# A vision tower on one core: values in stationaries of 32 or 64 columns dealt over strips, and half of the key spreading on ScalarE

## The reference

```python
q, k, v = split(x @ Wqkv)                 # H heads of d
att = softmax-like(q @ k.T * scale)       # 26 x 26 for each head
out = (att @ v) @ Wo                      # then added back
```

## Time and profile before

| | |
|---|---|
| median of three runs | 3102.24 us (3101.4 to 3104.73) |
| span of the profiled execution | 3102.3 us |
| TensorE busy | 2887.7 us, 93% |
| VectorE busy | 2090.0 us, 67% |
| ScalarE busy | 1075.2 us, 35% |
| GpSimd busy | 616.9 us, 20% |

### The profile page before, as it was taken

The page is one execution under the profiler, slowest core; times in us unless marked ns, Lnnn a source line. Parts: engine busy times, 40 slices in busy tenths (PEclk is TensorE's granted clock), DMA queues, the critical chain, the costliest instruction groups (busy, mean ns, idle before and its releaser), DMA issues. The chain is left out here.

```text
span 3102.3 us, 56416 instructions
## 1 busy us (share of the span) xinstructions
PE 2887.7 (93%) x19925; PEld 2668.6 (86%) x19925; DVE 2090.0 (67%) x5299; ACT 1075.2 (35%) x2140; POOL 616.9 (20%) x807
## 2 busy tenths in 40 slices
PE   8889999999999999999997998896989889958888
PEld 7789999999999999999997888675778889957677
DVE  3867677777777777777776766333457667777876
ACT  2533333333333333233333333212445333334433
POOL 1312121212112121212112110112213101122450
PEclk9989999999999999999998999798999889989898
DMA  3001100000000000000000000371000100000000
GB/s 136 36 20 37 37 21 33 36 36 18 36 36 36 18 36 36 24 30 36 18 31 9 2 2 2 117 237 54 2 11 2 54 19 19 1 11 16 23 19 17
DMA packets 24461, 105.56 MB, mean 34 GB/s; under 512 B 4455, under 2 KB 9463, under 8 KB 19086
## 3 DMA queue, kind: packets, MB, share of 16 engines
q1 hardware_dynamic: 22654, 99.62, 9.2%
q0 software_dynamic: 1584, 3.30, 0.3%
HBM read 98.32 MB, written 6.64 MB: 34 GB/s over the span
## 5 line engine op out<-in xcount | busy, mean ns | idle before, releaser
L905 ACT ACTIVATE hid<-bank,dat 128x384 f32<-128x384 f32 (+1 forms) x912 | 554.4, 608 | 1147.9 <-PE bank L595 1033.3
L870 PE MATMUL bank<-w,hid_hi 128*128 128x384 f32 x2964 | 857.5, 361 | 2.2 <-DVE y_tok L921 1.6
L872 PE MATMUL bank<-w,hid_lo 128*128 128x192 f32 x2964 | 745.0, 251 | 0.0
L872 PEld LDWEIGHTS bank<-w,hid_lo 128*128 128x128 f32 x2964 | 570.2, 192 | 1.7
L870 PEld LDWEIGHTS bank<-w,hid_hi 128*128 128x128 f32 x2964 | 560.8, 189 | 5.7 <-issue 4.1
L939 DVE TENSOR_TENSOR hid_lo<-hid,hid_hi 128x384 fp32r<-128x384 f32 (+1 forms) x912 | 540.0, 592 | 31.5
L936 DVE CAST hid_hi<-hid 128x384 fp32r<-128x384 f32 (+1 forms) x912 | 340.9, 374 | 126.7 <-ACT hid L905 125.4
L962 DVE SCALAR_TENSOR_TENSOR h_tok<-bank,gate,h_tok 128x192 f32<-128x192 f32 x416 | 173.6, 417 | 246.8 <-PE bank L872 243.3
L595 PE MATMUL bank<-xa_hi,w_hi 128*128 128x384 f32 (+1 forms) x912 | 324.6, 356 | 7.3 <-DVE w_lo L748 4.4
L595 PE MATMUL bank<-xa_lo,w_hi 128*128 128x384 f32 (+1 forms) x912 | 323.2, 354 | 0.0
L595 PE MATMUL bank<-xb,w_lo 128*128 128x384 f32 (+1 forms) x912 | 322.7, 354 | 0.0
(11 more groups left out here) (361 smaller groups left out, 4367.3 us busy)
## 6 DMA issues: line engine op xcount, KB each, us to landing
raw<-in_L_exp SPq DMA_DIRECT2D x36, 1344.0 KB, 5.7
w_e<-in_L_exp SPq DMA_DIRECT2D x20, 576.0 KB, 3.9
w_e<-in_L_exp SPq DMA_DIRECT2D x20, 384.0 KB
pix<-in_pixels SPq DMA_DIRECT2D x6, 832.0 KB, 10.3
w_e<-in_L_exp SPq DMA_DIRECT2D x20, 195.0 KB
raw<-in_L_mlp SPq DMA_DIRECT2D x2, 1344.0 KB, 6.5
wp_raw<-in_L_att SPq DMA_DIRECT2D x1, 2304.0 KB, 8.2
route_rows<-in_rows_clear SPq DMA_DIRECT2D x1, 2000.0 KB, 23.4
```

Source lines behind the costliest of these rows:

```text
L870: nc.tensor.matmul(o[:, 0:2 * D], hid_hi[k % 2][:, m, c], w2[j][:, m, :], start=m == 0, stop=False)
L872: ins = nc.tensor.matmul(o[:, 0:D], hid_lo[k % 2][:, m, c], w2[j][:, m, 0:D], start=False, stop=m == HC - 1)
L905: nc.scalar.activation(hid[(6 * k + m) % 3][:, 0:128 * nt], bank[4 + (6 * k + m) % 4][:, 0:128 * nt], func, bias=bias).then_inc(s["h_act"] ...
```

## The change

Four things.

1. `v_x` keeps a cell of `max(32, d)` columns for each head (32, in relative 64) in place of 128: with d = 16 two heads share 32 output rows, and each cell has its 16 values on its own side. A values instruction has a stationary of one cell and writes only the strip of output rows in which the head belongs, and neighbouring instructions go to different strips. The features of heads 8 to 11, which stand twice, are now computed twice: 16 instructions for 12 heads of 16 (before 12), 8 in causal (before 6), 24 in relative (before 18). The copy of the values into `v_x` is one instruction.
2. Scores and the relative offsets: the loop over chunks is the outer one, the loop over images (strips) the inner.
3. Half of a turn's key spreading, chunks NC/2 and up, moves from VectorE's `spread` to ScalarE, in two parts of three heads (`keys`), with a new semaphore `k_half` that the scores of the turn's first tile wait for. Causal keeps all of it on VectorE.
4. `v_x` is 1536 columns in place of 3200, and its clearing (GpSimd) shrinks with it.

```diff
-        v_x = sb("v_x", [128, 2 * 1536 + 128], scope=at)
+        v_x = sb("v_x", [128, 2 * 768], scope=at)
...
                 order += [("exp", 2, 0), ("bd", 1, 0), ("values", 0, 0), ("v", 2, 0), ("scores", 3, 0)] + kq
-                order += [("exp", 3, 0), ("bd", 2, 0), ("values", 1, 0), ("v", 3, 0)]
+                order += [("exp", 3, 0), ("bd", 2, 0), ("keys", 0, 1), ("values", 1, 0), ("v", 3, 0), ("keys", 1, 1)]
...
-                order = [("k", 0, 1), ("bd", 0, 0), ("mass", 0, 0), ("q", 0, 1), ("scores", 0, 1), ("values", 0, 0),
+                order = [("k", 0, 1), ("bd", 0, 0), ("mass", 0, 0), ("keys", 0, 1), ("q", 0, 1), ("keys", 1, 1), ("scores", 0, 1), ("values", 0, 0),
...
+            cell = max(32, d)
+            in_cell = cell // d
+
+            def value_cell(j, h):
+
+                x0 = 768 * j + cell * h
+                return v_x[:, x0:x0 + cell]
...
                     if g == 0:
                         pe.wait_ge(s["k_done"].sem, b["k_done"] + i + 1)
+                        if cfg.kind != "causal":
+                            pe.wait_ge(s["k_half"].sem, b["k_half"] + i + 1)
                         used(last_qk[0], i, last_qk[1])
                     o = bank[4 + g % 2]
-                    for im in range(4):
-                        m = SLOT * (4 * g + im)
-                        for c in range(NC):
-                            kx = key_rows(i, c * HCH, HCH).rearrange("p (h n) -> p h n", n=n)
+                    for c in range(NC):
+                        kx = key_rows(i, c * HCH, HCH).rearrange("p (h n) -> p h n", n=n)
+                        w = HCH * SLOT
+                        for im in range(4):
+                            m = SLOT * (4 * g + im)
                             q0 = qcols(c, i).start + m
-                            w = HCH * SLOT
...
-                    for im in range(4):
-                        m = SLOT * (4 * g + im)
-                        for c in range(NC):
+                    for c in range(NC):
+                        for im in range(4):
+                            m = SLOT * (4 * g + im)
                             ins = nc.tensor.matmul(o[32 * im:32 * im + 32, 40 * c:40 * c + 40],
...
-                    def product(o, h, start, stop):
-                        x0 = 1536 * (g % 2) + 128 * h
-                        return nc.tensor.matmul(o, v_x[:, x0:x0 + 128], p_bd[g % 2][:, h, :], start=start, stop=stop)
+                    def product(o, h, strip, start, stop):
+
+                        return nc.tensor.matmul(o[cell * strip:cell * strip + cell, :], value_cell(g % 2, h),
+                                                p_bd[g % 2][:, h, :], start=start, stop=stop)
...
-                            for c, hs in enumerate((range(H * 2 // 3), range(H * 2 // 3, H))):
-                                for h in hs:
-                                    ins = product(ob[:, 104 * c:104 * c + 104], h, h == hs[0], h == hs[-1])
+                            low_heads = H * 2 // 3
+                            for c in range(2):
+                                for y in range(in_cell):
+                                    for strip in range(4):
+                                        h = in_cell * strip + y if c == 0 else low_heads + in_cell * (strip % 2) + y
+                                        ins = product(ob[:, 104 * c:104 * c + 104], h, strip, y == 0, y == in_cell - 1)
...
-                                product(o, 2 * (3 * v + k), True, False)
-                                product(o, 2 * (3 * v + k) + 1, False, False)
+                                for u in range(2):
+                                    product(o, 2 * (3 * v + k) + u, u, True, False)
                                 part = rel_mass[g][:, 128 * c:128 * c + 128].rearrange("p (b s) -> p b s", s=32)
-                                ins = nc.tensor.matmul(o, rel_table[:, 128 * p:128 * p + 128], part[:, :, 0:SLOT],
-                                                       start=False, stop=True)
+                                for u in range(2):
+                                    r0 = 128 * p + 64 * u
+                                    ins = nc.tensor.matmul(o[64 * u:64 * u + 64, :], rel_table[:, r0:r0 + 64],
+                                                           part[:, :, 0:SLOT], start=False, stop=True)
...
+                key_heads = [(c, h) for c in range(NC // 2, NC) for h in range(HCH)]
+
+                def keys(i, part):
+
+                    m = len(key_heads) // 2
+                    for c, h in key_heads[m * part:m * part + m]:
...
+                        ins = nc.scalar.activation(key_rows(i, c * HCH + h, 1), k_chunk(c), ACT.Identity,
+                                                   scale=heads[:, h:h + 1])
+                    if part == 1:
+                        ins.then_inc(s["k_half"].sem, 1)
...
-                    for c in range(NC):
+                    for c in range(NC // 2):
```

More of the change, by code:

```diff
@@ L227, in vit_tower @@
                  "job_full", "job_used", "staged", "bd_zero", "bd_full", "bd_low", "qk_ready", "s_full", "s_used", "z_full", "p_full",
-                 "px_full", "av_full", "av_used", "t_full", "t_used", "out_done", "bridge", "k_done",
+                 "px_full", "av_full", "av_used", "t_full", "t_used", "out_done", "bridge", "k_done", "k_half",
                  "o_split", "it_dve", "holds", "root", "normed", "hi_full", "scale_full", "lo_full", "hi_step", "rel_table", "att_hi", "att_ready"]
@@ L1488, in attention @@
             b = base(job_full=len(jobs), job_used=len(jobs), staged=3 * 16, bd_zero=1, bd_full=16, bd_low=32, k_done=NI, s_full=16,
-                     s_used=16, z_full=16, p_full=16, px_full=16, av_full=16 * halves, av_used=16 * halves,
+                     s_used=16, z_full=16, p_full=16, k_half=0 if cfg.kind == "causal" else NI, px_full=16, av_full=16 * halves, av_used=16 * halves,
                      o_split=NI, it_dve=C * NI, qk_ready=4 * NI if cfg.kind == "causal" else 2 * NI, rel_table=5 * rel_kind, t_full=TILES, t_used=TILES)
@@ L1534, in attention, with value_spots @@
                     .rearrange("p (h n) -> p h n", n=104) for j in range(2)]
-            def spots(j, at, copies, copy_step, heads, step):
-                part = v_x[:, 1536 * j + at:1536 * j + at + 1]
-                return bass.AP(part.tensor, part.offset, [part.ap[0], [copy_step, copies], [step, heads], [1, d]])
+            cell = max(32, d)
[3 more added lines that the diff above has]
+                return v_x[:, x0:x0 + cell]
+            def value_spots(j, h0, heads):
+                part = value_cell(j, h0)[:, 0:1]
+                return bass.AP(part.tensor, part.offset, [part.ap[0], [cell * in_cell, heads // in_cell],
+                                                          [cell + d, in_cell], [1, d]])
             def sync(sp):
@@ L1867, in projections @@
                                 ins.then_inc(s["qk_ready"].sem, 1)
+                key_heads = [(c, h) for c in range(NC // 2, NC) for h in range(HCH)]
+                def keys(i, part):
+                    m = len(key_heads) // 2
+                    for c, h in key_heads[m * part:m * part + m]:
+                        if h == 0 or (c, h) == key_heads[m * part]:
+                            last = ("fk", i, c) if cfg.kind == "performer" else ("qk", i, qk.index(("k", c)))
+                            act.wait_ge(s["job_used"].sem, b["job_used"] + at[last] + 1)
+                        ins = nc.scalar.activation(key_rows(i, c * HCH + h, 1), k_chunk(c), ACT.Identity,
+                                                   scale=heads[:, h:h + 1])
+                    if part == 1:
+                        ins.then_inc(s["k_half"].sem, 1)
                 def features(i, f):
@@ L1884, in value_projection @@
                             act.wait_ge(s["av_full"].sem, b["av_full"] + halves * (t - 1))
-                        if no == 2:
-                            low_heads = H * 2 // 3
-                            ph = p.rearrange("p (u h d) -> p u h d", u=1, d=d)
-                            nc.scalar.activation(spots(j, 0, 1, 0, low_heads, 128 + d), ph[:, :, 0:low_heads, :],
-                                                 ACT.Identity)
-                            ins = nc.scalar.activation(spots(j, 128 * low_heads, 2, 64, H - low_heads, 128 + d),
-                                                       ph[:, :, low_heads:H, :].to_broadcast([128, 2, H - low_heads, d]),
-                                                       ACT.Identity)
-                        else:
-                            ph = p.rearrange("p (k u d) -> p u k d", u=2, d=d)
-                            ins = nc.scalar.activation(spots(j, 768 * v, 2, 192, 3, 256), ph, ACT.Identity)
-                        ins.then_inc(s["job_used"].sem, 1)
+                        nc.scalar.activation(value_spots(j, HH * v, HH), p.rearrange("p (k u d) -> p k u d", u=in_cell, d=d),
```

(3 more changed lines are left out.)

## The result

The changed kernel takes 3024.5 us (median of four runs, 3012.25 to 3028.76) against 3103.36 before on the same chip: ratio 0.9741, 95% interval 0.9719 to 0.9763. It is 79 us faster; 118 were forecast. The forecast of 2984 us is 40 too low, and the result lies inside the range of 2930 to 3035.

The account below looks back on a forecast made before the run. TensorE, busy for 93% of the 3102.2 us, was taken as the bound, with VectorE second. Gains by phase summed to 135 us, less 17 for the clock: net 118, so 2984 us, range 2930 to 3035.

Parts of the forecast that it names:

- rivals 1 and 4: Rival 1: half clock most of each turn, 3025 us, chance 0.16; rival 4: run-ahead sets overlap, scores gain nothing, 3027, 0.08.
- The strips: TensorE values groups 1.9 us less on 64 tiles; 16 performer score tiles 1.0 off, 16 relative 1.7; causal values 0.75 off.
- Keys: Half of a turn's key multiplications moved to ScalarE: VectorE's 4.61 us falls to 2.3, with a new wait for scores.
- The prediction's turns: Turn lengths after the change: performer 27.4 us, softmax 19.0, log2 21.2, mixing 25.3, relative 29.1; causal 0.9 off a turn.
- DVE the bound: Softmax and log2 turns: VectorE nearly full after the change, at turns of 19 and 21 us.
- The given back 1.3 to 1.5 us: Softmax turn: VectorE waits 1.3 to 1.5 us a turn for scores held up behind ScalarE's keys and copies.
- A turn times four: Phases of four turns: the drain is counted as a turn, since it holds as many values groups; performer four turns, 39 us.
- The clock: 24 turns, all but performer: TensorE waits more and its clock falls, 0.7 us each, 17 us given back.
- Rival 2: All attention phases: the waits vanish and only engine time counts, 176 us gained, 2926 us; chance 0.12.
- Rival 3: TensorE strips with stationaries of all 128 rows do not overlap in accumulation groups: +49 us, about 3151; chance 0.02.
- the marks for "wrong": Signs against the forecast: values over 1.5 us, softmax turns above 21 us, or granted clock in these phases under 0.85.

Follow-up runs that it names:

- e1_no_keys: The change without its third part, all key multiplications of a turn back on VectorE: 2993.1 us, ratio 0.9639.
- e9_half_free: The change with no keys on ScalarE, and from a phase's second turn on half of VectorE's key multiplications left out, done by nobody: 2974.4 us, ratio 0.9581.

## Why the prediction was right, and where it was off

The direction and two mechanisms were right: strips overlap once they are dealt, and part 3 brings a wait. The size was not: 79 us came of 118. That 3024.5 lies in the range of 2930 to 3035 is in part luck, since its upper end was set that high for rivals 1 and 4, and neither happened as described.

**The strips: right.** 0.86 for 0.80 us, 2.29 for 2.14, 0.57 for 0.6, 1.27 for 1.3. Entering narrow stationaries costs 0.09 us again (0.20 from the last wide start at 2306.66 us to the scores at 2306.86, and 0.11 between wide ones). Leaving them costs more than that: 0.86 less eight rounds of 0.089 is 0.15, and in the earlier trace rows the scores' 0.69 less four rounds of 0.13 is 0.17, which the prediction called a change of width without giving it this price. The Trainium skill ("TensorEngine Tiling (Array Packing)", section "Key Properties") says that a change of tiling mode drains the engine; these rows agree, with those prices. Its factor for three column strips (the Trainium skill, "TensorE: Matmul & The Clock Gate", section "Part 3: Packing small matmuls"), scaled to four, would have made 0.99 with the change of width; 0.86 lies between that and the full four, nearer to the full.

**Keys: right in three phases, wrong in softmax and log2.** The prediction's turns hold 2.3 us of VectorE saved in softmax, log2 and mixing against 1.2 to 1.5 us given back, and 1.2 to 1.4 paid in relative and performer. Over the phases that nets 5.6 (performer) + 9.6 (relative) - 3.2 (softmax) - 3.6 (log2) - 2.7 (mixing) = a cost of 6 us. Measured 31, and 25 of the 39 us missed are this. By phase, the change against e1_no_keys in the profiles: relative 9.5 dearer (9.6 forecast), performer 3.2 (5.6), mixing 3.4 cheaper (2.7), but softmax 6.2 dearer and log2 9.4, where gains of 3.2 and 3.6 were forecast. Three steps failed:
- "DVE the bound" in softmax and log2: in e9_half_free 3.4 us a phase came off for the 6 to 7 that three half spreads take. In mixing they came off whole, as said.
- The given back 1.3 to 1.5 us counted one late arrival a turn. Runs show two costs, ScalarE's time (28 us, most of it in softmax and relative) and the wait (23 us, most of what the profiles show of it in log2), 51 over 24 turns: 2.1 a turn. The 0.26 us by which three multiplications were taken too short is the small part of it.
- The stretch ahead of a phase's first scores was not looked at. There both parts of the keys stand bare: from before to the change it grew from 12.8 to 14.2 us in softmax, 9.5 to 11.1 in log2, 14.0 to 18.0 in mixing and 21.8 to 23.4 in performer.

**A turn times four: wrong.** The other 14 us are in the strips' share (124 by the prediction's turns without the keys, 110 measured). Nearly all of them are performer's, 33.9 us gained where 46.4 were put; outside it the phases without the keys fell 19 us short of their turns, about the 17 set aside for the clock. The prediction took performer's third turn for every turn, the drain included. Between first scores, its turns were 30.2, 36.6, 37.3 and then 35.3 to the end; without keys they are 24.3, 26.3, 26.9 and 28.1. That is 5.9, 10.3, 10.4 and 7.2 gained where 11.6 was put four times. The first and the last turn before:

```profile
2165.20:2195.40 30.20, 29.48 (x248) 21.89 (x249) 14.00 (x36) 13.17 (x33) 6.76 (x20) 1.00 0.00 1
2269.40:2304.70 35.30, 32.06 (x333) 29.90 (x332) 19.15 (x59) 12.36 (x30) 5.67 (x14) 1.00 0.00 1
```

In the first turn TensorE is as full as later (29.5 of 30.2 us), but only two of the phase's sixteen values groups stand in it (48 records). The last holds six, worth 11.4 us, and gains least for its groups: without the keys TensorE is busy for 21.8 of its 28.1 us, waits for copies and split outputs, and runs at a granted clock of 0.82. So the drain has the groups, as the prediction says, but TensorE doesn't bound it.

**The clock: right in direction.** Half-clock time doubled, from 80 to 164 us, as the 17 us said. Their size is not confirmed: in log2 the clock went up with no gain, in causal and in performer's last stretch 2 to 3 us go with it. Rival 1 (half clock for most of each turn, 3025 us) names nearly the time that came out, yet by another cause: 164 us are 19% of the 853 us of the phases, and the run without the keys has 178 and is 31 us faster.

Rival 2 was wrong in that the waits did not vanish; its 2926 us lie below even e9_half_free's 2974. Rival 3 fell with values groups of 0.86 us. Of the marks for "wrong", two were touched: one softmax turn stands at 21.4 us, and the granted clock was under 0.85 in causal, log2 and mixing turns (0.82, 0.74, 0.76).

## What to carry to other kernels

Deal small matmuls over the strips, in the inner loop: it gave 0.86 us for 2.70 here, near the full factor of four a round, though four heads are computed twice. An engine at half load is no free place for work if copies that others wait for stand behind it in its order: price the move by what is queued behind it and by the new wait, each apart, and look at the stretch ahead of the first turn, where nothing covers it. Before costing a turn "times four", read all four turns, and in the drain ask who bounds it.

## What the runs showed of the hardware

An ACTIVATE from SBUF to SBUF with a scale that is read from a tile takes 632 ns (mean) for 96x416, and three in a row 1.71 us; `Square` with no such operand takes 534 ns (median) in the kernel before, and four in a row 1.87 us. From start to start that is 0.54 and 0.45 us. For 128x208 it took 457 ns against 344 for a copy out of PSUM. In the first pair the place of the source is the same and function and operand differ, in the second the place and the operand; which of them costs isn't shown.

Eight records in a row on one 32-column strip before the next strip's, 128x104: 1.97 us for 32; dealt over four strips: 0.86. Going from 128-column to 32-column stationaries costs about 0.09 us, going back about 0.15, an estimate from rounds of 0.089.
